# Shorter vector instructions in the first layer's edge loop of a four-layer graph network

## The reference

```python
# layer 0, attention over the edges (4 heads of 16)
g = leaky_relu(xl[src] + xr[dst] + edge_attr_16 @ W_e, 0.2)
logits = einsum('ehc,hc->eh', g, att)
alpha = exp(logits - amax[dst]) / (denom[dst] + 1e-16)
out = segment_sum(xl[src] * alpha, dst)          # then batch norm, + x, gelu
# layer 1: four steps of  neigh = segment_sum(emb[src], dst...)
# layer 2: one message sum with edge_attr_64
# layer 3: two hops of a normalised neighbour sum, then a product
```

## Time and profile before

| What | Value |
|---|---|
| Median of 3 runs | 8234.38 us (8220.6 to 8267.23) |
| Span of the profiled execution, first to last instruction | 6576.8 us |
| Busy in the span: PE, DVE, ACT, POOL | 5007.3, 3022.6, 1799.8, 3882.2 us |
| The edge loop within the span | 430 to about 2853 us |
| Mean granted clock of PE in the edge loop | 0.85 |
| Mean share of the DMA engines in the edge loop | 0.55 |

### The profile page before, as it was taken

How to read it: one execution, slowest core, us unless ns; L and a number is a source line. 1 busy time by engine, 2 the same in 40 slices (tenths; PEclk the granted TensorE clock), 3 DMA queues, 4 the chain that set the end, 5 groups by cost and what they waited for, 6 DMA issues and landing times. The chain is left out here.

```text
span 6576.8 us, 115590 instructions
## 1 busy us (share of the span) xinstructions
PE 5007.3 (76%) x35178; PEld 4266.4 (65%) x35178; DVE 3022.6 (46%) x3931; ACT 1799.8 (27%) x3844; POOL 3882.2 (59%) x3427
## 2 busy tenths in 40 slices
PE   2338888888888888841999957877878787771898
PEld 2315665665566655531999957777777777771898
DVE  7757777777777777746322131111111111113322
ACT  0024555555555545510000012222222222220000
POOL 5748788888788888750000047777777777773000
PEclk9668888888888888955999955555555555555898
DMA  9335555555555555522999846666666666652895
GB/s 358 77 84 141 151 153 152 143 150 150 154 155 146 150 149 154 153 61 84 329 366 366 312 128 202 204 203 203 205 204 203 206 204 197 202 178 62 336 389 215
DMA packets 659138, 1262.13 MB, mean 192 GB/s; under 512 B 167881, under 2 KB 467466, under 8 KB 633268
## 3 DMA queue, kind: packets, MB, share of 16 engines
q1 hardware_dynamic: 381076, 726.95, 32.8%
q10 hardware_dynamic: 168480, 416.21, 18.9%
q0 software_dynamic: 109184, 115.05, 9.8%
HBM read 924.66 MB, written 490.51 MB: 215 GB/s over the span
## 5 line engine op out<-in xcount | busy, mean ns | idle before, releaser
L696 POOL DMA_INDIRECT att_gl<-tab_l,att_ix x1568 | 1933.5, 1233 | 487.6 <-issue 472.3
L1184 POOL DMA_INDIRECT sum_gl<-tab_l,sum_ixs x1568 | 1572.3, 1003 | 524.7 <-issue 477.8
L937 ACT ACTIVATE att_acc<-att_pc 128x392 bf16<-128x392 f32 x2352 | 1083.3, 497 | 1324.1 <-PE att_pc L715 1122.6
L712 PE MATMUL att_pc<-att_ohl,att_ohv 128*128 128x392 bf16 x2352 | 863.0, 367 | 272.0 <-DVE att_ohl L812 271.7
L1134 PE MATMUL sum_pm<-sum_msg,sum_S 128*128 128x64 f32 x3136 | 680.0, 407 | 425.6 <-ACT sum_msg L1158 425.5
L1134 PEld LDWEIGHTS sum_pm<-sum_msg,sum_S 128*128 128x128 f32 x3136 | 647.0, 314 | 465.7 <-issue 264.7
L715 PE MATMUL att_pc<-att_acc,att_ohv 128*128 128x392 bf16 x2352 | 855.7, 364 | 116.3 <-ACT att_acc L937 112.7
L1104 DVE TENSOR_TENSOR sum_t<-sum_pb,sum_gl 128x512 f32<-128x512 f32 x196 | 135.6, 692 | 1692.1 <-DMA sum_gl<-tab_l,sum_ixs 1692.1
L1116 PE MATMUL sum_pb<-sum_wbs,sum_ea 64*128 64x64 f32 x3136 | 694.5, 419 | 27.4 <-DMA sum_ea<-in_ea64T 27.4
L731 PEld LDWEIGHTS att_pl<-att_xe,att_S 128*128 128x128 f32 x3136 | 599.3, 216 | 159.8 <-issue 137.3
L1116 PEld LDWEIGHTS sum_pb<-sum_wbs,sum_ea 64*128 64x128 f32 x3136 | 676.1, 329 | 39.0 <-DMA sum_ea<-in_ea64T 27.6
(11 more groups left out here) (360 smaller groups left out, 5190.2 us busy)
## 6 DMA issues: line engine op xcount, KB each, us to landing
A<-att_acc SPq DMA_DIRECT2D x2352, 98.0 KB
l_a<-A SPq DMA_DIRECT2D x147, 1568.0 KB, 9.2
l_at<-AT SPq DMA_DIRECT2D x98, 1568.0 KB
att_dall<-in_dst ACTq DMA_DIRECT2D x224, 448.0 KB
sum_dall<-in_dst SPq DMA_DIRECT2D x196, 512.0 KB, 4.8
sum_a<-A SPq DMA_DIRECT2D x49, 1568.0 KB, 10.1
AT<-sum_at ACTq DMA_DIRECT2D x49, 1568.0 KB, 5.4
tot<-att_o ACTq DMA_DIRECT2D x56, 1022.0 KB
```

The source lines that it names most:

```text
L696: nc.gpsimd.indirect_dma_start(out=gl[s][:, c, :], out_offset=None, in_=g.tab_l, in_offset=bass.IndirectOffsetOnAxis(ap=ix[s][:, c:c + 1], ...
L712: nc.tensor.matmul(pc[c][m % 2][:, 0:LO], ohv[c][h][:, m, :, 0], ohl[c][h][:, m // 2, :, m % 2], start=True, stop=False)
L937: nc.scalar.activation(acc[c][n % CR][:, :], pc[c][m % 2][:, 0:LO], ACT.Copy).then_inc(s_acc[c], 1)
L1184: nc.gpsimd.indirect_dma_start(out=gl[q][:, j, :], out_offset=None, in_=g.tab_l, in_offset=bass.IndirectOffsetOnAxis(ap=ixs[q][:, j:j + 1] ...
```

## The change

Both edits lie in DVE's program of `edge_loop`. In `same`, the comparison of 7 chunks becomes two instructions, of 4 and of 3 chunks. In `items`, the one-hots of a step's 6 or 4 items, until now one instruction for `ohv` and one for `ohl`, are made two items at a time: 3 or 2 instructions for each. The waits stay ahead of the first instruction, and the semaphore is incremented by the last of each group. The tiles, their types and what is written to them stay as they are.

```diff
                     dve.wait_ge(s_dall[k], i * (16 * R) + (16 * s + 16))
-                    v.tensor_tensor(S[s][:, k * GQ:(k + 1) * GQ, :], dall[k][:, :, :],
-                                    spread(dst[:, bass.ds(i * (R * GB) + t * GQ, GQ)].unsqueeze(2), [P, GQ, P]),
-                                    ALU.is_equal).then_inc(s_S, 1)
+                    for a, z in ((0, 4), (4, GQ)):
+                        ins = v.tensor_tensor(S[s][:, k * GQ + a:k * GQ + z, :], dall[k][:, a:z, :],
+                                              spread(dst[:, bass.ds(i * (R * GB) + (t * GQ + a), z - a)].unsqueeze(2),
+                                                     [P, z - a, P]), ALU.is_equal)
+                    ins.then_inc(s_S, 1)
...
-                    v.tensor_tensor(ohv[c][h][:, 0:w, :, :], spread(c_row2[:, :, :].unsqueeze(1), [P, w, P, 2]),
-                                    spread(g.vals[:, bass.ds(n0, w), :].unsqueeze(2), [P, w, P, 2]), ALU.is_equal)\
-                        .then_inc(s_oh[c], 1)
-                    v.tensor_tensor(ohl[c][h][:, 0:w // 2, :, :], spread(c_lo2[:, :, :].unsqueeze(1), [P, w // 2, LO, 2]),
-                                    spread(g.lo[:, bass.ds(n0, w)].rearrange("p (j two) -> p j two", two=2).unsqueeze(2),
-                                           [P, w // 2, LO, 2]), ALU.is_equal).then_inc(s_oh[c], 1)
+                    for m in range(0, w, 2):
+                        ins = v.tensor_tensor(ohv[c][h][:, m:m + 2, :, :],
+                                              spread(c_row2[:, :, :].unsqueeze(1), [P, 2, P, 2]),
+                                              spread(g.vals[:, bass.ds(n0 + m, 2), :].unsqueeze(2), [P, 2, P, 2]),
+                                              ALU.is_equal)
+                    ins.then_inc(s_oh[c], 1)
+                    for m in range(0, w, 2):
+                        ins = v.tensor_tensor(ohl[c][h][:, m // 2, :, :], c_lo2[:, :, :],
+                                              spread(g.lo[:, bass.ds(n0 + m, 2)].unsqueeze(1), [P, LO, 2]),
+                                              ALU.is_equal)
+                    ins.then_inc(s_oh[c], 1)
```

## The result

The changed kernel is slower: 8400.26 us at the median of 4 runs (8354.78 to 8410.77), against 8245.03 of the kernel before (8220.6 to 8267.23), a ratio of 1.0151 with a 95% interval of 1.0088 to 1.0215. The forecast was 8084.

A forecast was written before the change was run, and what follows sets the result against it. The prediction took POOL's gathers, held by DVE instructions, to bound the first layer's edge loop. Span 6577 us, less 150 gained, plus 1658 around it, made 8084 us; the range for 8 in 10 was 8010 to 8205.

The forecast's parts named there:

- the sum: Whole kernel: span 6577 us, less 150 gained, plus 1658 taken to lie around the span, makes 8084 us.
- POOL never stands still for anybody: First layer's edge loop: POOL's busy time, issue and 15 us of real waits make up the loop's 2421 us.
- a gain of 150 us: Edge loop: 216 us back on POOL, 180 after DVE's remaining idle time, less 30 for TensorE's slow-clock stretches.
- The pieces: DVE in the edge loop: shortened instructions take 420 and 561 ns for one-hots, 690 and 556 for destinations.
- an extra instruction: DVE in the edge loop: each costs 70 ns because neighbours overlap; 1680 of them cost 118 us.
- The holds: Gathers in the edge loop: time held by DVE falls from 451 to 235 us, giving POOL 216 us back.
- The mechanism of the hold: A gather is held until the DVE instruction in progress ends, then needs 0.82 us; unheld it takes about 0.945 us.
- Rival 3: DVE in the edge loop: extra instructions cost 0.153 us without overlap, 83 us slower, 8317 us; 5%.
- Rival 2: Gathers in the edge loop: holds don't shrink, time stays 8234 us; with gathers holding DVE, together 9%.
- Rival 4: TensorE in the edge loop: longer at its lower clock, slower from a mean of about 0.81 down; 4%.
- Rival 1: Edge loop: DVE or TensorE takes over early, a gain of 41 to 80 us, 8154 to 8193 us; 12%.

The follow-up runs named there:

- the second profile: The kernel before, unchanged, profiled once more: span 8210.6 us in an execution of 8212.36 us.
- the kernels that wait for landing: POOL waits after each 7 gathers until they have landed: added to the kernel before 7563.87 us (0.9155), to the changed kernel 7612.68 us (0.9235).
- the paused kernel: The changed kernel with POOL waiting after each 7 gathers until they have landed: 7612.68 us, 0.9235 of before; 7310 to 7450 us was expected.

## Why the prediction was wrong

**The step that failed** is the sum: "1657.6 us lie around the span, and nothing of that is touched". They don't lie around it. In a timed execution 1.8 us do; the rest is within the span, 1162 us of it in the edge loop (3572 for 2410). With that step the first one falls too, "POOL never stands still for anybody": true of the profile that was read, whereas in the second profile it stands 1482 us for messages and indices. So a shorter gather did not shorten the loop: in place of a gain of 150 us the gathers gave back 62 us and the waits took 200, and the loop is 138.9 us longer. The signs were there: a span 20% shorter than every run was taken for a remainder that needs no explanation.

**Right by its own steps.** The pieces: 418 and 559 ns (420 and 561 forecast), 692 and 552 for the destinations (690 and 556). Three pieces of `ohv` take 1.09 us where one instruction took 0.953, so an extra instruction costs 0.07 us, as forecast, and DVE is busy 112 us more in the loop (118). The Trainium skill's fixed cost of 151 cycles (VectorE: DVE Perf Modes, "The TRN2 errata"), 157 ns, agrees with the 153 ns that the rows give for one instruction by itself. As the price of one more, which made 264 us of it, the trace does not bear it out, because the next piece starts before the one ahead has ended. And by the run with 1680 small memsets the count of instructions was not what mattered. The holds shrink, from 150 to 88 us, to 0.59 of what they were (235 of 451, 0.52, forecast): in the kernels that wait for landing from 444 to 247, by 197 us for the 216 forecast, though POOL no longer sets the pace in the changed one. (The working lets a gather lose u - 0.125 us and then sums with 0.155; with 0.125 throughout the forecast is 196.) The mechanism of the hold was read rightly. Its sign for the time was not.

**The rivals.** Rival 3, the only slower one by DVE, has the wrong cause: the same number of instructions costs nothing when they don't change the holds. Rival 2 is out, the holds shrank. Rival 4, the clock, did not decide: 0.69 is below the 0.81 that was named as its sign, but before the change it is 0.70 in the second profile. Rival 1 would have left the time below before's. None of the five had late increments in it. The kernel did get slower, as rivals 3 and 4 had it, but by neither of their causes.

**What is shown and what is open.** Shown: increments are late for work that ends while gathers are being issued, and none is without gathers; where POOL has waits left, lengthening its bursts by pauses takes 2 us or more off them for each us; it is the shorter instructions that lose time and not their number, and each of the change's two parts does so by itself. In four comparisons the waits rose by about 3 us for each us of hold that was lost. Only argued: that the lost hold is what makes them rise. Against it stand fixed pauses that did not give the loss back, a forecast that failed for the paused kernel, and the low count of increments recorded during holds. It may be that the short instructions do something else during a burst; DVE instructions shortened without a change of the holds were not tried. Also open is what holds the increments up, and why the execution profiled first was free of it.

**The version to use** of those tried is the kernel before with 1.2 us of idle POOL work for every 7 gathers, in one piece or in two: 7330 to 7354 us beside 8251.79, a ratio of 0.888 to 0.893, and 0.883 on another chip, some 11% less time.

## What to carry to other kernels

If a profile's span is far from the runs' time, profile again before anything is summed: that remainder is time that the trace doesn't explain. Where one engine issues gathers in long bursts and another engine's wait says "remote", break the bursts with a short pause and see if the whole gets faster; how much pause is worth it ends where the issuing engine has no waits left. And before you remove a stall on one engine, count what the others wait for: here the stall became shorter, as forecast, and the whole slower.

## What the runs showed of the hardware

While indirect gathers are issued back to back (0.94 us each, 0.30 us apart), semaphore increments of TensorE come 4.0 us late at the median and over 19 us late in one case of ten, while its matmuls themselves had run; while POOL waits, 0.014 us. Gaps of 1.2 us every 7 gathers bring the median down to 0.3 to 0.6 us. ACT's loads were not late in the same way: on the queue that carries them the next packet moved 0.63 us after the issue at the median, during bursts, outside them and in the profile read first. The same kernel also had an execution in which none of this was seen, with a loop of 2410 us instead of 3572.

Instructions of one column added to a DVE that stands still for over 1500 us of its loop cost nothing that can be measured here: 1680 of them, 59 ns each, changed the time by 0.04% (interval -0.45 to 0.54%).
